# Value products placed ahead of the transposes of the second next tile in TensorE's loop over row tiles

## The reference, cut to what matters

```
xn = _layernorm(x, axis=-1)
x = x + _L1_gnn_ref(xn, edge_index, ...) + _L1_mix_ref(xn[None], ...)[0]
...
# in _L1_gnn_ref
qkv = x @ W_qkv.T + b_qkv
Q, K, V = jnp.split(qkv, [DK * HEADS, 2 * DK * HEADS], axis=-1)
...
# in _L1_mix_ref
qkv = x @ w_qkv.T
q, k, v = jnp.split(qkv, 3, axis=-1)
q = jax.nn.softmax(q, axis=-1)
k = jax.nn.softmax(k, axis=-2)
```

## Time and profile before

| | us |
|---|---|
| median of three runs | 2181.97 |
| lowest and highest of them | 2178.82, 2182.57 |
| the profiled execution | 2182.49 |
| its span, from the first to the last instruction | 2180.8 |
| mean granted TensorE clock in it (1.0 is full) | 0.944 |

### The profile page before, as it was taken

How to read it: one execution, slowest core, us unless ns; L and a number is a source line. 1 busy time by engine, 2 the same in 40 slices (tenths; PEclk the granted TensorE clock), 3 DMA queues, 4 the chain that set the end, 5 groups by cost and what they waited for, 6 DMA issues and landing times. The chain is left out here.

```text
span 2180.8 us, 30949 instructions
## 1 busy us (share of the span) xinstructions
PE 1929.8 (88%) x10068; PEld 1079.3 (49%) x10069; DVE 1317.8 (60%) x3826; ACT 738.5 (34%) x1747; POOL 772.0 (35%) x849
## 2 busy tenths in 40 slices
PE   8999898898987988977768999699999876999997
PEld 5343433343443434433233554477777445777775
DVE  5866798898898898898644235376676422111111
ACT  0111344444444444433221133256666211222221
POOL 0000577777777777777600000111111000212111
PEclk9999999999999998989889999899999976999999
DMA  5001699999999999999940136744531243334441
GB/s 161 12 24 65 257 397 408 391 397 403 398 401 401 395 404 406 386 393 398 381 152 0 48 105 204 218 128 136 149 115 63 73 160 129 92 102 115 150 149 29
DMA packets 143181, 479.65 MB, mean 220 GB/s; under 512 B 16590, under 2 KB 17262, under 8 KB 142800
## 3 DMA queue, kind: packets, MB, share of 16 engines
q0 software_dynamic: 99952, 353.16, 43.0%
q1 hardware_dynamic: 43104, 124.95, 17.2%
HBM read 445.93 MB, written 32.11 MB: 219 GB/s over the span
## 5 line engine op out<-in xcount | busy, mean ns | idle before, releaser
L599 POOL DMA_INDIRECT m_ring<-in_table,m_rows_at x640 | 651.0, 1017 | 221.0 <-issue 140.5
L960 PE MATMUL m_acc<-m_ring,m_diag 64*64 64x512 f32 x2560 | 428.6, 680 | 121.1 <-ACT m_diag L776 120.9
L659 DVE CUSTOM_DVE_ANT_0 m_ring<-m_ring,m_coming,m_part 128x512 f32<-128x512 f32 x640 | 442.8, 749 | 44.1 <-DMA m_ring<-in_table,m_rows_at 33.7
L960 PEld LDWEIGHTS m_acc<-m_ring,m_diag 64*64 64x64 f32 x2560 | 136.5, 146 | 377.9 <-ACT m_diag L776 282.7
L776 ACT ACTIVATE m_diag<-m_eye,m_inner 128x64 f32<-128x64 f32 x640 | 222.0, 347 | 280.0 <-DVE m_inner L659 279.7
L2100 PEld LDWEIGHTS e_psU<-e_rowsT,x_w 128*128 128x128 f32 x1472 | 171.9, 196 | 14.3 <-issue 14.3
L1595 DVE CUSTOM_DVE_ANT_0 a_prob<-a_psS,xnT 128x1250 f32<-128x1250 f32 x80 | 116.8, 1460 | 102.0 <-PE a_psS L1532 102.0
L2100 PE MATMUL e_psU<-e_rowsT,x_w 128*128 128x128 f32 x1472 | 172.3, 279 | 3.0 <-DMA x_w<-in_we 1.9
L2109 PE MATMUL e_psY<-x_w,e_hT 128*128 128x512 f32 x368 | 161.7, 592 | 0.0
L1532 PE MATMUL a_psS<-a_k,a_q 128*128 128x512 f32 (+1 forms) x480 | 116.3, 378 | 21.0 <-DMA a_k<-qk_parts 16.7
L1518 POOL DMA_DIRECT2D a_q<-qk_parts x80 | 42.9, 537 | 257.2 <-PE a_psS L1532 256.9
(11 more groups left out here) (347 smaller groups left out, 2744.4 us busy)
## 6 DMA issues: line engine op xcount, KB each, us to landing
x_w<-in_we SPq DMA_DIRECT2D x16, 2048.0 KB, 10.4
xnT<-edge_log_counts SPq DMA_DIRECT2D x40, 640.0 KB, 4.0
m_ring<-in_table,m_rows_at POOLq DMA_INDIRECT x640, 6.8
qk_parts<-t_parts SPq DMA_DIRECT2D x32, 320.0 KB, 4.4
a_k<-qk_parts SPq DMA_DIRECT2D x32, 320.0 KB, 9.6
edge_log_counts<-t_log_cnt SPq DMA_DIRECT2D x10, 640.0 KB, 3.5
a_q<-qk_parts POOLq DMA_DIRECT2D x80, 64.0 KB, 2.1
edge_counts<-cnt SPq DMA_DIRECT2D x10, 320.0 KB, 2.1
```

The costliest lines, as they stand in the source:

```text
L599: pool.indirect_dma_start(ring[:, slot, :], None, ins["table"], bass.IndirectOffsetOnAxis(rows_at[:, h, k:k + 1], 0)).then_inc(s_land[slot ...
L659: dve.tensor_tensor_reduce(ring[:, slot, 0:D], ring[:, slot, 0:D], coming[:, t % 2, :], part[:, b, k:k + 1], 0.0, ALU.mult, ALU.add, inner ...
L960: mm = pe.matmul(acc[to, i, :], diag[rows, h % 2 * TOPK + k, :], ring[rows, nth % RING, D:2 * D], start=h == 0 and k < 2, stop=h == HEADS ...
```

## The change

In pass t of the loop, TensorE gets `values(t)` directly behind `queries(t)`, and `turn(t + 2)` behind both. Nothing else is different: no instruction is added or taken away, and the four other engines have the same streams.

```diff
             turn(1)
             for t in range(NT):
                 queries(t)
+                values(t)
                 if t + 2 < NT:
                     turn(t + 2)
-                values(t)
             pe.wait_ge(s["xout"], NT)
```

## The result

| | before | changed |
|---|---|---|
| median | 2180.69 us (4 runs) | 2158.24 us (4 runs) |
| lowest and highest | 2178.82, 2182.57 | 2155.80, 2158.95 |
| the profiled execution | 2182.49 | 2155.80 |
| its span | 2180.8 | 2153.9 |

The ratio of the times is 0.9894, with a 95% interval of 0.9882 to 0.9907: the changed kernel is 22.5 us faster (20.3 to 25.7 by the interval). The forecast was 2159.1, a gain of 22.8 on the 2181.97 us of the first three runs of the kernel before; a fourth run has moved its median to 2180.69.

The account below looks back on a forecast made before the run. TensorE was taken as the bound, held up in the loop by waits for VectorE's normalised rows. Waits 16.0, slow stretches 5.1 and overlap with shorter transposes 1.7 sum to 22.8 us gained: 2159.1 us, range 2154.2 to 2165.9.

Parts of the forecast that it names:

- The waits: In the loop, TensorE's eight 2.0 us waits at the transposes for VectorE's normalised rows go, gaining 16.0 us.
- The step on the cover: Rows ready about 2.1 us after the values start, TensorE reaching the transposes at 3.43: 1.3 us of cover per pass.
- The pace: A loop pass without waits takes 6.87 us, read from passes 8 and 9, plus 0.44 for transposes in a running stream.
- The clock: In the loop, the granted clock no longer falls behind the waits; three slow stretches go, gaining 5.1 us.
- slow stretches: Loop passes whose values run mostly at the 1.2 GHz level, 5.30 us instead of 3.60; each makes the pass 1.69 us dearer.
- Rival A: The loop's clock falls all the same, from another cause; three falls remain, 17.8 us gained, 2164.2 us; chance 7%.
- The first pass: Tile 0's values start 0.17 us before its queries end, 2.68 us ahead of before, their weights landed 4 us in time.
- What passes on: Behind the loop TensorE stays the bound to 1374, so the gain shifts everything later; key product at about 1179.
- the sum: The last values start at 1174.27 instead of 1197.11, 22.8 us gained: 16.0 waits, 5.1 slow stretches, 1.7 overlap and shorter transposes.
- Rival D: Later stages have one or two low-clock stretches more or fewer, up to 3.4 us either way; inside the forecast's 88%.
- B: VectorE becomes the loop's bound; at 8.4 us per VectorE pass 9 us of gain are lost, 2168 us; chance 3%.
- Rival C: The whole loop without waits runs throttled at 1.2 GHz, 41 us slower, 2223 us; chance 1%.

## Why the prediction was right

**The waits.** Forecast 16.0 us; all eight are gone. The step on the cover is shown in two ways: 1.3 us in the timeline, and a wait of 1.00 us when the rows were made some 2.4 us later.

**The pace.** Forecast 6.87 + 0.44 us for a pass and 65.35 from the first to the last values; measured 65.31. The pace of the new order was rightly read from passes 8 and 9, which already had it.

**The clock.** Forecast 5.1 us for three slow stretches; filling the idleness bought 4.8 and 6.1 us in the two filler kernels. Their intervals are 2.8 to 7.6 and 3.3 to 8.1 us, so the term is confirmed in sign and rough size; the 5.1 itself was read from a single execution, and how many slow stretches the other runs of the kernel before had is not recorded. Rival A had 7% and is refuted by the two. The page of the Trainium skill that stood beside it (TensorE: Matmul & The Clock Gate, "Why this matters for your kernels") names longer gaps as those that cost the clock. In this kernel gaps of 2.0 us did it, in three of eight cases and in two of four, so the measurement decides against taking the rule as a bound.

**The first pass.** The values of tile 0 were to start 0.17 us before the queries' end, without a wait for their weights. They do (1101.97 + 4.25 is 1106.22, and the values start at 1106.06). What was not foreseen is the length of tile 0's queries: 5.77 us in the profiled execution of before, 4.25 after, and between 4.21 and 5.70 in the experiments, since the clock rises within them: it was 0.50 from 1103 to 1107 us in the execution of before, and 1.00 from 1104 us on in that of the changed kernel. From one execution to another that is 1.5 us, and no part of the change.

**What passes on.** From the first transposes to the key product it was 100.51 us and is 76.12, 24.39 less: 22.84 of the sum and 1.51 of those queries leave 0.04. From the key product to the end of the span it was 978.9 us and is 977.7. Rival D was given 3.4 us either way, and one pair of executions shows 1.2. The key product was forecast for about 1179 and came at 1176.19; besides the 1.51, the stage itself began 1.4 us earlier. These explain why the two profiled executions lie 26.7 us apart and the medians 22.5. That the medians came within 0.3 us of the gain forecast is partly luck: the interval of the measured gain is 5 us wide.

**The rivals B and C.** VectorE ends its pass 2.8 us ahead of its next maxima, so it isn't the bound. In none of the executions whose TensorE waited 1.15 us or less did the clock fall below 1.00 in the loop behind tile 0's queries. Rival C, the loop throttled without waits, is refuted by the same clock of 1.00.

Open is why a wait of 2.0 us lowers the clock in some passes and not in others. The runs show only that it isn't settled by the length of the wait alone, nor needs the waits to lie close together. In the kernel before the falls lie behind every second wait (1120.63, 1141.39 and 1162.14, but not 1182.88), and with half of the passes changed they lie behind the first and the third of four. Two executions don't tell whether that is a pattern or chance.

## What to carry to other kernels

Where an in-order engine waits for another in the middle of a loop, look for an instruction behind it in its queue that needs nothing of what is awaited, or for one ahead of the awaited instruction on the other engine that needn't be there: either edit gave the whole gain here. The two together were not run; after either one no wait is left in the loop for the other to remove. Price the clock with the wait, since eight idle spells of 2.0 us cost 5 us on top of their own 16. And if the tail of a loop already runs in the planned order, its pace is a good forecast of the new loop: 65.35 us forecast here, 65.31 measured.

## What the runs showed of the hardware

- Idle spells of TensorE, in a loop of passes with 7 to 9 us of matmuls, and the low stretches behind them, in one profiled execution of each kernel: at 0.29, 1.00 and 1.15 us none of eight each, at 2.0 us three of eight and two of four, at 4.43 us eight of eight. The same 8.0 us of idleness in one loop lowered the clock twice in spells of 2.0 us and never in spells of 1.0.
- Replacing idleness by products that nobody reads made the kernel faster, by 4.8 us (0.9976, 0.9965 to 0.9987) and 6.1 us (0.9974, 0.9963 to 0.9985).
- One slow stretch costs 1.4 to 1.7 us: 5.30 us instead of 3.60 for a tile's values, or 1.1 and 4.9 for transposes and values instead of 0.66 and 3.60. The low end is pass 0 of the kernel with doubled waits, 1.11 and 4.58.
